# A message-passing layer with residual and layer norm on one core: deeper gather rings, single split buffers, a new order of the first stage and paced clears

## What is computed

```python
h = x @ W_in2f
Wij = (ssp(edge_attr @ Wf1 + bf1) @ Wf2 + bf2) * edge_weight     # ssp(z) = softplus(z) - log 2
m = segment_sum(h[dst] * Wij, src, num_segments=50000)
m = ssp(m @ Wo1 + bo1) @ Wo2 + bo2
out = layernorm(x + (x + m))
```

## Time and profile before

| what | value |
|---|---|
| median of three runs | 1863.84 us (1859.76 to 1867.15) |
| the profiled execution | 1858.28 us |
| its span, first to last instruction | 1856.5 us |
| busy PE / PEld / DVE / ACT / POOL | 91 / 83 / 80 / 80 / 78 % |
| mean granted TensorE clock | 0.972 |
| DMA | 363.47 MB, 196 GB/s over the span |

### The profile page before, as it was taken

How to read it: one execution, slowest core, us unless ns; L and a number is a source line. 1 busy time by engine, 2 the same in 40 slices (tenths; PEclk the granted TensorE clock), 3 DMA queues, 4 the chain that set the end, 5 groups by cost and what they waited for, 6 DMA issues and landing times. The chain is left out here.

```text
span 1856.5 us, 36676 instructions
## 1 busy us (share of the span) xinstructions
PE 1697.3 (91%) x11376; PEld 1532.2 (83%) x11376; DVE 1489.3 (80%) x3750; ACT 1492.9 (80%) x2945; POOL 1441.4 (78%) x1385
## 2 busy tenths in 40 slices
PE   3499899999999999999999998889976999999995
PEld 2378788888888888888888887778866999999995
DVE  2477788787888888888888786777765999999996
ACT  2477788778888788888888786776756999999996
POOL 7422488888887888878888888888754999999997
PEclk9699999999999999999999998999998999999998
DMA  9799866656566665666665666665675999999994
GB/s 354 251 356 372 266 123 112 126 112 125 115 125 122 112 123 114 124 125 112 125 120 116 119 122 113 114 118 108 116 185 170 333 363 362 360 360 364 357 366 174
DMA packets 177341, 363.47 MB, mean 196 GB/s; under 512 B 25622, under 2 KB 76264, under 8 KB 177148
## 3 DMA queue, kind: packets, MB, share of 16 engines
q1 hardware_dynamic: 101128, 257.75, 39.8%
q0 software_dynamic: 75136, 102.45, 32.4%
q10 hardware_dynamic: 884, 0.92, 0.2%
HBM read 206.90 MB, written 154.12 MB: 194 GB/s over the span
## 5 line engine op out<-in xcount | busy, mean ns | idle before, releaser
L354 POOL DMA_INDIRECT acc<-sums,src_ix x392 | 637.2, 1626 | 141.6 <-issue 116.0
L341 POOL DMA_INDIRECT xg<-in_x,dst_t x392 | 401.4, 1024 | 215.6 <-issue 114.6
L780 DVE SCALAR_TENSOR_TENSOR m_l<-pair,wgt_t,m_h 128x256 fp32r<-128x256 f32 x392 | 171.6, 479 | 230.5 <-ACT m_h L621 206.6
L385 POOL TENSOR_SCALAR sums<-sums,neg_mean,rstd 128x256 f32<-128x256 f32 x392 | 283.2, 733 | 10.2
L495 PE MATMUL pair<-m_h,same 128*128 128x256 f32 (+1 forms) x980 | 244.8, 285 | 30.4 <-ACT sums L628 21.9
L621 ACT ACTIVATE m_h<-pair,wgt_t 128x256 fp32r<-128x256 f32 x392 | 165.0, 475 | 99.5 <-PE pair L409 57.6
L495 PE MATMUL pair<-m_l,same 128*128 128x256 f32 (+1 forms) x980 | 241.8, 281 | 0.0
L409 PE MATMUL pair<-wo_h,msg_h 128*128 128x256 f32 (+1 forms) x784 | 230.9, 295 | 6.0 <-DVE m_l L780 5.2
L495 PEld LDWEIGHTS pair<-m_h,same 128*128 128x128 f32 (+1 forms) x980 | 185.1, 189 | 52.2 <-issue 34.9
L576 ACT ACTIVATE zs<-pair,bf 128x512 f32<-128x512 f32 x196 | 124.1, 685 | 125.8 <-PE pair L433 99.5
L409 PE MATMUL pair<-wo_h,msg_l 128*128 128x256 f32 (+1 forms) x784 | 222.0, 283 | 0.0
(11 more groups left out here) (97 smaller groups left out, 5249.8 us busy)
## 6 DMA issues: line engine op xcount, KB each, us to landing
acc<-fill SPq DMA_DIRECT2D x197, 256.0 KB
xg<-in_x SPq DMA_DIRECT2D x97, 512.0 KB, 6.4
sums<-acc SPq DMA_DIRECT2D x97, 512.0 KB, 6.8
out<-sums SPq DMA_DIRECT2D x97, 512.0 KB, 4.7
attr<-in_edge_attr SPq DMA_DIRECT2D x196, 128.0 KB
...
```

The lines of the kernel that those rows point to most:

```text
L341: pool.indirect_dma_start(xg[0:g.p, g.xs, r], None, t["x"], bass.IndirectOffsetOnAxis(ap=dst_t[0:g.p, r, g.n:g.n + 1], axis=0)).then_inc(x ...
L354: pool.indirect_dma_start(acc, bass.IndirectOffsetOnAxis(ap=src_ix[g.slot][0:g.p, r:r + 1], axis=0), sums[0:g.p, g.slot, r], None, compute ...
L385: last = pool.tensor_scalar(normed[0:g.p, g.n % NRING, r], res[0:g.p, u, r], neg_mean[0:g.p, u, r:r + 1], rstd[0:g.p, u, r:r + 1], ALU.add ...
L780: dve.scalar_tensor_tensor(out=m_l[0:g.p, r], in0=bank[6][0:g.p, k * D:(k + 1) * D], scalar=col(wgt_t, r, g), in1=m_h[0:g.p, r].bitcast(F3 ...
```

## The change

The change has six parts.

1. The rings are deeper: XRING 11 to 17, RING 12 to 14, and POOL gathers AHEAD = 30 groups instead of 23 before its first scatter.
2. `x_h`, `x_l`, `ssp_h`, `ssp_l` and `same` have one buffer instead of two, and `ssp` and `msg` are gone: `softplus` and `message` write their result back into the PSUM bank that they read, and both split parts are taken from there. So a bank is free for PE only after the low part is taken: `filter1` waits for `sspl_sb`, `w_of` for `msgl_sb`.
3. The three lists have a new order and shorter lags: for instance `absolute`, `expo`, `loga` and `softplus` come in the same step as `filter1` (lag 0, before 1), `compare` is cut into four stages, and `summed(0)` and `keep_y` move one step forward.
4. SP waits before each clear until the clear four places before it has landed (IN_FLIGHT = 4). The early wait for the first gather is gone.
5. `fetch_x` for the second stage is issued inside the loop of the first stage, group by group, and not after it.
6. The tiles that DMAs write or read (`sums`, `xg`, `attr`, `srcb`, `fill`) are allocated first, at multiples of 128 bytes; small tables share space. In the second stage `ssp2` lies in `sums`, and the split parts of odd groups lie in `x_h`, `x_l`.

```diff
-RING = 12
-XRING = 11
+RING = 14
+XRING = 17
-AHEAD = 23
-EARLY_CLEARS = 8
+AHEAD = 30
 FIRST_CLEARS = 36
+IN_FLIGHT = 4
 CLEARS_A_STEP = 16
...
+        sums = sb("sums", [P, RING, R, D])
+        xg = sb("xg", [P, XRING, R, D])
+        attr = sb("attr", [P, ARING, ROWS])
+        srcb = sb("srcb", [P, SRING, ROWS], I32)
+        fill = sb("fill", [P, CLEAR, D])
         ident = sb("ident", [P, P])
...
-        x_h, x_l = (sb(n, [P, 2, H, R, P], F32R) for n in ("x_h", "x_l"))
-        zs, ssp = (sb(n, [P, H, 512]) for n in ("zs", "ssp"))
-        ssp_h, ssp_l = (sb(n, [P, 2, H, R, P], F32R) for n in ("ssp_h", "ssp_l"))
-        same = sb("same", [P, 2, R * (R + 1) // 2, P], F32R)
-        h_sb, msg = (sb(n, [P, H, 512]) for n in ("h_sb", "msg"))
+        x_h, x_l = (sb(n, [P, H, R, P], F32R) for n in ("x_h", "x_l"))
+        zs, h_sb = (sb(n, [P, H, 512]) for n in ("zs", "h_sb"))
+        ssp_h, ssp_l = (sb(n, [P, H, R, P], F32R) for n in ("ssp_h", "ssp_l"))
+        same = sb("same", [P, R * (R + 1) // 2, P], F32R)
-        ssp2, ssp2_h, ssp2_l = [ssp, msg], ssp_h, ssp_l
+        ssp2 = [sums[:, MRING + DEPTH + NRING + k].rearrange("p r d -> p (r d)").rearrange("p (h n) -> p h n", h=H) for k in range(2)]
+        ssp2_h, ssp2_l = [ssp_h, x_h], [ssp_l, x_l]
...
+        cleared = [sem(f"cleared{u}") for u in range(IN_FLIGHT)]
...
             def clear_to(count):
                 for c in range(clears, min(count, CLEARS)):
-                    sp.dma_start(acc[c * CLEAR * P:(c + 1) * CLEAR * P, :].rearrange("(p k) d -> p (k d)", k=CLEAR), fill[:, 0:CLEAR].rearrange("p k d -> p (k d)")).then_inc(cleared, 16)
+                    a, b = c * CLEAR * P, min((c + 1) * CLEAR * P, N + R * P)
+                    wait(sp, cleared[c % IN_FLIGHT], c // IN_FLIGHT * 16)
+                    sp.dma_start(acc[a:b, :].rearrange("(p k) d -> p (k d)", k=CLEAR),
+                                 fill[0:(b - a) // CLEAR].rearrange("p k d -> p (k d)")).then_inc(cleared[c % IN_FLIGHT], 16)
-            clear_to(EARLY_CLEARS)
-            sp.wait_ge(xg_in[0], 16 * R)
             clear_to(FIRST_CLEARS)
...
             for n in range(2, G + 1):
                 if n < G:
                     load_attr(n)
                 load_src(n - 1)
                 clear_to(FIRST_CLEARS + (n - 1) * CLEARS_A_STEP)
+                if G - XRING <= n - 2:
+                    fetch_x(group((n - 2) % XRING))
...
-                wait(pe, ssp_sb, g.n * H)
+                wait(pe, sspl_sb, g.n * H)
-                    wait(pe, msg_sb, g.n * H + m)
+                    wait(pe, msgl_sb, g.n * H + m)
-            run((w_of(1), 2), (summed(0), 3), (h_of(0), 1), (summed(1), 3), (filter1, 0), (turn_x(0), 0),
-                (out1(0), 2), (turn_x(1), 0), (w_of(0), 1), (h_of(1), 1), (out1(1), 2), before={1: filter_bias})
+            run((w_of(1), 2), (summed(1), 3), (turn_x(0), 0), (turn_x(1), 0), (out1(0), 2), (h_of(0), 1), (filter1, 0),
+                (w_of(0), 1), (out1(1), 2), (h_of(1), 1), (summed(0), 2), before={1: filter_bias})
...
-                    high(ssp_h[:, g.par, h], ssp[:, h].rearrange("m (r e) -> m r e", r=R), ssph_sb)
+                    high(ssp_h[:, h], bank[2 + h][:].rearrange("m (r e) -> m r e", r=R), ssph_sb)
-                    high(msg_h[:, m], msg[:, m].rearrange("f (r e) -> f r e", r=R), msgh_sb)
+                    high(msg_h[:, m], bank[5][:].rearrange("f (r e) -> f r e", r=R), msgh_sb)
-            run((keep_y(0), 4), (msg_high(1), 3), (ssp_high(0), 2), (ssp_high(1), 2), (keep_h(0), 2), (absolute(0), 1),
-                (absolute(1), 1), (expo(0), 1), (m_high(0), 3), (keep_y(1), 4), (expo(1), 1), (x_high(0), 1), (loga(0), 1),
-                (loga(1), 1), (x_high(1), 1), (keep_h(1), 2), (m_high(1), 3), (a_high, 0), (msg_high(0), 2), before={1: weights})
+            run((x_high(0), 1), (keep_y(0), 3), (x_high(1), 1), (ssp_high(0), 1), (msg_high(1), 2), (ssp_high(1), 1), (keep_y(1), 3),
+                (a_high, 0), (m_high(0), 2), (keep_h(0), 1), (absolute(0), 0), (absolute(1), 0), (expo(0), 0), (expo(1), 0),
+                (loga(0), 0), (loga(1), 0), (msg_high(0), 1), (m_high(1), 2), (keep_h(1), 1), before={1: weights})
...
-                    wait(dve, msgl_sb, (g.n - 1) * H + m + 1)
-                    dve.scalar_tensor_tensor(out=msg[:, m], in0=bank[5][:], scalar=bias_w[:, m:m + 1], in1=h_sb[:, m],
+                    dve.scalar_tensor_tensor(out=bank[5][:], in0=bank[5][:], scalar=bias_w[:, m:m + 1], in1=h_sb[:, m],
-                    dve.scalar_tensor_tensor(out=ssp[:, h], in0=bank[2 + h][:], scalar=neg_bf1[:, h:h + 1], in1=zs[:, h],
+                    dve.scalar_tensor_tensor(out=bank[2 + h][:], in0=bank[2 + h][:], scalar=neg_bf1[:, h:h + 1], in1=zs[:, h],
-            run((m_low(0), 3), (message(0), 2), (x_low(0), 1), (softplus(0), 1), (softplus(1), 1), (x_low(1), 1),
-                (m_low(1), 3), (message(1), 2), (a_low, 0), (msg_low(0), 2), (target, 3), (msg_low(1), 2), (ssp_low(0), 1),
-                (ssp_low(1), 1), (compare, 2), before={1: first_weights, 2: tables, 3: second_weights})
+            run((x_low(0), 1), (message(1), 2), (x_low(1), 1), (msg_low(1), 2), (ssp_low(0), 1), (ssp_low(1), 1), (a_low, 0),
+                (compare(0), 2), (m_low(0), 2), (compare(1), 2), (compare(2), 2), (message(0), 1), (compare(3), 2), (softplus(0), 0),
+                (msg_low(0), 1), (softplus(1), 0), (m_low(1), 2), (target, 2),
+                before={0: biases, 1: first_weights, 2: tables, 3: second_weights})
```

121 lines of the change are left out of this document (58 added, 63 removed).

## The result

The changed kernel takes 1905.4 us (1904.0 to 1906.4) against 1862.7 us: 1.0227 times as long, 95% interval 1.0204 to 1.0249. The prediction was 1857 us with a range from 1818 to 1885. The profiled execution has a span of 1902.3 us, 45.8 more than before.

A forecast was written before the change was run, and what follows sets the result against it. It took POOL's gathers and scatters to bound the first stage's last part, TensorE its middle, ScalarE the second stage. 1858.3 - 9 (clears) + 4 (middle) - 2 (end) = 1851, plus 0.3%: 1857 us, range 1818 to 1885.

The forecast's parts named there:

- paced clears and the start: Start of first stage: with four clears in flight, `attr` of group 12 goes out at 197 us, 9 us earlier.
- Deeper rings, 30 groups ahead: First stage: POOL needs 11.74 us a group instead of 12.15, its part ends 38 us earlier and is no longer the bound.
- The clears become slow: Rival, start: paced clears slower than 0.91 us each delay `attr`; at 1.0, +11 us, median 1877; chance 0.13.
- that rival's worst case: Start: at 1.2 us a clear, `attr` of group 12 goes out at 255 us, total 1915.
- four in flight: Start: with four clears in flight, ScalarE's waits such as 10.02 us were expected to shrink.
- The middle: First stage, groups 12 to 97: steps of 13.4 us against 13.35, +4 us over 85 steps.
- The circle: Middle of first stage: waits through TensorE, ScalarE and VectorE from one `out1(0)` to the next, 13.2 us a step.
- the 0.17 that was added for stalls: Middle steps: TensorE's present idle time per step, added to 13.2 us, giving 13.4.
- where `keep_y` was forecast: Sign that the forecast is right: POOL waits for `keep_y` in the second half.
- The end and alignment: First stage's end: new lags save about 2 us after the last `filter1`; DMA tiles at 128-byte multiples: zero.
- The nine transactions for eight: Rival on alignment: clears fall from 0.81 to 0.72 us, -18 us, median 1839; chance 0.07.
- The one that named stalls on the circle: Rival, middle: with single buffers ScalarE or VectorE stalls delay all; 13.7 us a step, median 1883; chance 0.14.

The follow-up runs named there:

- gate13: Changed kernel with POOL's first run of gathers cut to its earlier length, rings and 30 groups ahead kept: 1881.5 us, 1.0083 of the kernel before.
- unpaced: Changed kernel with clears issued without waiting for the clear four places before: 1894.7 us, 1.0152 of the kernel before.
- target_later: Changed kernel with VectorE's `target` moved behind `a_low`, a step later: 1909.8 us, 1.0231 of the kernel before.

## Why the prediction failed, step by step

**The failed step: paced clears and the start.** The prediction read the ten-us waits of the earlier trace rows as caused by the clears that went out beside them, and let them shrink: -9 us. They came from the gathers. The step that should have cost this is the first part, "Deeper rings, 30 groups ahead": it priced only what POOL saves later, and held that "the first scatter still comes at step 12 or a little later". It did come at step 12, but at 269.9. What was missed is that six more slots are six more groups in a run without a pause, and that the start of ScalarE's operations in the earlier trace rows can be set against the end of the work waited for. Then the waits are seen to be released one by one until some ten us after POOL's run ends. The runs that bear on the price: a run of gathers of the old length gives back 24 us of the 42.7 (gate13), unpaced clears 10.7 (unpaced). The two were not taken out together in one run with 30 groups ahead, so that they add up to the loss is not shown.

**Pacing, the right rival with the wrong cause.** "The clears become slow" had break-even at 0.91 us a clear; after, 16 take 13.6 us, 0.85, without counting the first 52, which took 1.2 and more. It costs 10.7 us, inside its price, where the sum had 9 us of gain, and does not reach 1905 alone. That `attr` of group 12 goes out at 261.3, close to the 255 of that rival's worst case, is luck: there each clear was to take 1.2 us, and for 40 us SP stood for TensorE's results, not for clears. The prediction's sentence "four in flight" as a cure had no row behind it.

**The middle: right in size, in part by luck.** 13.4 us was forecast, and it is 1141.4 / 85 = 13.43. The circle is closed as the prediction traced it, and its 13.2 us are the 13.19 of the later steps. But the 0.17 that was added for stalls came from TensorE's idle time before; what lengthened the steps was 0.27 us from 478 to 1019 us and nothing later, and between 478 and 1019 us the mean did not follow the circle when it was made shorter. VectorE and ScalarE in one undisturbed step after, in order of time:

```profile
1238.12 0.59 ACT L557 ACTIVATE msg_h<-pair 128x512 fp32r<-128x512 f32 x1
...
1242.45 0.60 ACT L557 ACTIVATE msg_h<-pair 128x512 fp32r<-128x512 f32 x1 [0.58 <-DVE pair L767]
```

```profile
1238.74 0.69 DVE L674 TENSOR_TENSOR msg_l<-pair,msg_h 128x512 fp32r<-128x512 f32 x1 [0.34 <-ACT msg_h L557]
1239.35 0.75 DVE L792 SCALAR_TENSOR_TENSOR pair<-pair,neg_bf,zs 128x512 f32<-128x512 f32 x1
...
1241.66 0.75 DVE L767 SCALAR_TENSOR_TENSOR pair<-pair,bias_w,h_sb 128x512 f32<-128x512 f32 x1
...
1243.08 0.69 DVE L674 TENSOR_TENSOR msg_l<-pair,msg_h 128x512 fp32r<-128x512 f32 x1
```

```profile
1230.64 0.39 PE L411 MATMUL pair<-wo_h,msg_h 128*128 128x256 f32 x1
...
1243.83 0.39 PE L411 MATMUL pair<-wo_h,msg_h 128*128 128x256 f32 x1
```

From `out1(0)` to the next is 13.19 us; from `msg_low(0)` to `message(1)` 2.92 (2.96 worked out), from there to `out1(0)` 2.17 (2.06 and a hand-off). TensorE, ScalarE and VectorE hand over within 0.06 us. The two writes to PSUM cost nothing: `message` takes 0.75 and `msg_low` 0.69 us, as 0.75 and 0.68 in the earlier trace rows. The price that the Trainium skill's table of the errata would have added ("VectorE: DVE Perf Modes", section on the TRN2 errata), 0.065 us for each low part taken from PSUM, does not show.

**POOL: right.** TensorE no longer waits for gathers in the end (the earlier trace rows has no counterpart), POOL waits from group 70 on (for `src_ix` of `target`, where `keep_y` was forecast), and from its first scatter it needs 11.63 us a group up to group 70, worked out as 11.74.

**The end and alignment: right.** -3.0 against -2; the second stage unchanged; alignment at zero. The nine transactions for eight of the Trainium skill ("DMA: Bandwidth & Descriptors", section on how a descriptor splits) would, as an estimate, have made some 12% of each clear; the run with shifted tiles shows nothing of that size in the time.

**The rivals.** The one that named stalls on the circle had the right sign and 13.7 us a step; the loss came before the circle began to turn. No rival had the run of gathers.

What stays open is by what way POOL's run holds back TensorE's results. The rows show a matmul's start and a modelled end, and the start of the operation that waits for it. The Trainium skill ("Perfetto Trace Analysis", section on Tensor Engine Instruction) says that TensorE's end in a trace is an estimate, and that its semaphore goes up only after PSUM has acknowledged the writing. The traces show that the time passes before the semaphore goes up. In target_later all four waits are marked `remote`, that is, ended by an event of the semaphore with no instruction of that moment that raises it (ScalarE, ScalarE, VectorE, ScalarE):

```profile
69.98 0.60 ACT L605 ACTIVATE h_sb<-pair 128x512 f32<-128x512 f32 x1 [44.05 <-remote]
81.33 1.26 ACT L578 ACTIVATE zs<-pair,bf 128x512 f32<-128x512 f32 x2 [10.74 <-remote]
97.50 0.76 DVE L767 SCALAR_TENSOR_TENSOR pair<-pair,bias_w,h_sb 128x512 f32<-128x512 f32 x1 [62.87 <-remote]
111.42 0.60 ACT L605 ACTIVATE h_sb<-pair 128x512 f32<-128x512 f32 x1 [12.54 <-remote]
```

The events of the semaphores, which TensorE alone raises, stand in that trace at 69.96, 81.30, 97.40 and 111.40 us, and the matmuls that raise them end, by the model, at 36.24, 37.17, 38.56 and 73.62. So ScalarE and VectorE are not slow to see them; the raising itself is late. Whether the matmuls are late or the way from them to the semaphore, no run here shows. Nor is a part of the recording ruled out: every execution on record was profiled, and of the first three of these events in the changed kernel's own trace none was kept.
